# A decoder's state-space layer: channels projected once, the convolution as shifted taps on ScalarE and VectorE

## What is computed

```python
zxbcdt = x @ W_in.T
z, xBC, dt_raw = zxbcdt[..., :512], zxbcdt[..., 512:1280], zxbcdt[..., 1280:]
y = causal_conv(xBC, conv_w)          # per channel, 4 taps: positions t-3 .. t
xBC = y * sigmoid(y)
xs, B, C = xBC[..., :512], xBC[..., 512:640], xBC[..., 640:]
dt = softplus(dt_raw + dt_bias); cum = cumsum(-exp(A_log) * dt)
M[i, j, h] = (C_i . B_j) * exp(cum_i - cum_j) * dt_j      # j <= i, 64 heads of 8
y = einsum(M, xs) + D * xs
y = rms_norm(y * silu(z)) * norm_w
return y @ W_out.T
```

## Time and profile before

| | |
|---|---|
| median of 3 runs | 2465.02 us (2462.78 to 2465.8) |
| the profiled execution | 2466.13 us, its span 2464.3 us |
| PE / DVE / ACT / POOL busy over the span | 83% / 68% / 54% / 51% |
| mean granted clock of PE | 0.954 |
| state space | from about 1017.8 to 1482.5 us of the span |

### The profile page before, as it was taken

The page is one execution under the profiler, slowest core; times in us unless marked ns, Lnnn a source line. Parts: engine busy times, 40 slices in busy tenths (PEclk is TensorE's granted clock), DMA queues, the critical chain, the costliest instruction groups (busy, mean ns, idle before and its releaser), DMA issues. The chain is left out here.

```text
span 2464.3 us, 36286 instructions
## 1 busy us (share of the span) xinstructions
PE 2053.8 (83%) x10114; PEld 1341.9 (54%) x10114; DVE 1665.6 (68%) x3834; ACT 1322.8 (54%) x5017; POOL 1253.8 (51%) x1524
## 2 busy tenths in 40 slices
PE   0776999999999997498888870499999999999995
PEld 0453666566656655255555440266666666666664
DVE  7454566676676675466565658367888877888886
ACT  1223566666666664223232323277777777777773
POOL 0014444444454442155555564156777766777765
PEclk9997999999999999699999995699999999999998
DMA  5000000000000002000000005000000000000000
GB/s 198 0 0 16 5 3 3 4 2 2 4 2 2 2 0 74 1 1 0 0 0 0 0 0 197 15 3 3 6 8 6 5 7 5 5 7 5 3 5 8
DMA packets 30027, 37.35 MB, mean 15 GB/s; under 512 B 3281, under 2 KB 24273, under 8 KB 29265
## 3 DMA queue, kind: packets, MB, share of 16 engines
q1 hardware_dynamic: 29904, 36.11, 4.3%
HBM read 34.00 MB, written 2.10 MB: 15 GB/s over the span
## 5 line engine op out<-in xcount | busy, mean ns | idle before, releaser
L1092 POOL TENSOR_TENSOR ssm_y<-ssm_y,ssm_term 128x512 f32<-128x512 f32 x112 | 142.2, 1269 | 146.7 <-DVE ssm_term L1265 144.2
L1593 POOL TENSOR_TENSOR fa_rs<-fa_rs,all_minus_half 128x4 f32<-128x4 f32 x192 | 197.9, 1031 | 15.0
L1654 PE MATMUL fa_pJB<-fa_w_kvx,fa_ctxT 128*128 128x512 f32 x256 | 128.7, 628 | 80.0 <-DMA fa_ctxT<-in_ctxT 79.3
L1778 ACT ACTIVATE fa_qT<-fa_pH,fa_head_vec 128x512 f32<-128x512 f32 x128 | 99.5, 777 | 173.7 <-PE fa_pH L1753 173.7
L1787 ACT ACTIVATE fa_pS<-fa_pS,fa_nb 128x128 f32<-128x128 f32 x512 | 182.6, 392 | 7.1 <-issue 6.7
L1590 POOL TENSOR_TENSOR fa_rs<-fa_ms,all_eps5w 128x4 f32<-128x4 f32 x192 | 43.9, 229 | 242.1 <-ACT fa_q_junk L1771 129.6
L1673 PEld LDWEIGHTS fa_pS<-fa_kT,fa_qT 128*128 128x128 f32 x1024 | 123.9, 191 | 65.3 <-ACT fa_qT L1778 58.5
L1614 POOL TENSOR_TENSOR fa_cat<-fa_ov,fa_om 128x512 bf16<-128x512 f32 x128 | 153.7, 1200 | 5.3
L1673 PE MATMUL fa_pS<-fa_kT,fa_qT 128*128 128x128 f32 x1024 | 148.2, 288 | 2.5 <-ACT fa_qT L1778 0.9
L1607 POOL TENSOR_TENSOR fa_ov<-fa_ob,fa_om 128x512 f32<-128x512 bf16 x128 | 147.7, 1154 | 4.7 <-DVE fa_om L1960 4.7
L521 PE MATMUL xa_pS<-xa_kT,xa_qT 128*128 128x256 f32 x512 | 126.2, 388 | 23.2 <-ACT xa_kT L699 17.5
(11 more groups left out here) (329 smaller groups left out, 5971.3 us busy)
## 6 DMA issues: line engine op xcount, KB each, us to landing
faw_raw<-in_fa_w SPq DMA_DIRECT2D x12, 512.0 KB, 6.7
faw_raw<-in_fa_wproj SPq DMA_DIRECT2D x8, 512.0 KB, 3.9
all_X<-in_x SPq DMA_DIRECT2D x1, 2048.0 KB, 13.5
shared_weights<-in_xa_wq SPq DMA_DIRECT2D x1, 2048.0 KB, 13.4
xa_wo<-in_xa_wo SPq DMA_DIRECT2D x1, 2048.0 KB, 18.3
xa_ctxT<-in_ctxT SPq DMA_DIRECT2D x16, 128.0 KB, 2.1
fa_w_kvx<-in_fa_wkvx SPq DMA_DIRECT2D x1, 2048.0 KB, 14.8
fa_ctxT<-in_ctxT SPq DMA_DIRECT2D x16, 128.0 KB, 2.1
```

The lines of the kernel that those rows point to most:

```text
L1092: pool.tensor_tensor(y[:, side, :], y[:, side, :], term[:, in_turn(side, l), :], ALU.add)\
L1593: pool.tensor_tensor(rs[:, j % 2, cols], rs[:, j % 2, cols], env.mhalf[:, cols], ALU.pow)\
```

## The change

B, C and x are projected once, all with channels on partitions: two products a tile of 128 channels (`channels`, 2 tiles into `pC`, 4 into `pX`). ACT writes the newest tap of each tile from PSUM to a new SBUF tile `conv`, scaled by a value per channel (`first_tap`); DVE adds the three older taps, each a multiply-add of the PSUM tile, read 1 to 3 positions earlier, into `conv` (`tap`: 3 steps of 2 tiles for B and C, 3 steps of 4 tiles for x, each step behind a semaphore of the one before). ACT takes Silu of B and C from `conv` to `bcT`. x is transposed back by PE into `pX` (4 transposes) and goes through Silu as before. `w_tap`, its four multiplications, the copy `cur`, the zero columns and their clearing go; x is transposed straight from `env.X`. On PE z's product moves ahead of C.B, between levels 1 and 2. On DVE the taps of B and C stand ahead of term 2, those of x behind it, and C.B's masks behind term 3. The steps are written out, with no loop. The tap weights are loaded as [128, 6, 4] (12 KB) in place of a copy on each partition (1536 KB).

```diff
-            steps(0, 0, False, True)
-            steps(1, 1, True, True)
-            with eng.Fori(2, B - 1, 2) as m:
-                steps(m, 0, True, True)
-                steps(m + 1, 1, True, True)
-            steps(B, 0, True, False)
+            for m in range(B + 1):
+                steps(m, m % 2, m > 0, m < B)
...
+                    def channels(bank, tiles):
+                        for n, tile in enumerate(tiles):
+                            for k in range(KT):
+                                last = pe.matmul(bank[:, n * P:(n + 1) * P], w_raw[:, k, tile * P:(tile + 1) * P],
+                                                 xT[:, k, :], start=(k == 0), stop=(k == KT - 1))
+                        return last
...
-                        for half in range(2):
-                            for n in range(TAPS * KT):
-                                t, k = n // KT, n % KT
-                                last = pe.matmul(pC[:, half * N:(half + 1) * N],
-                                                 w_tap[:, t, k, HID + half * N:HID + (half + 1) * N],
-                                                 xT[:, k, t:t + P],
-                                                 start=(n == 0), stop=(n == TAPS * KT - 1))
-                        last.then_inc(s["bc_ps"], 1)
+                        channels(pC, (4, 5)).then_inc(s["bc_ps"], 1)
+                        pe.wait_ge(s["xs_in"], now(m, 0))
+                        channels(pX, (0, 1, 2, 3)).then_inc(s["xp_ps"], 1)
                     next_level()
+                    next_level()
+                    if front:
+                        for k in range(KT):
+                            last = pe.matmul(pZ[:, :], xT[:, k, :], w_z[:, k, :],
+                                             start=(k == 0), stop=(k == KT - 1))
+                        last.then_inc(s["z_ps"], 1)
                     next_level()
...
-                    for n in range(TAPS * KT):
-                        if n in (0, 2, 4, 5, 6):
-                            next_level()
-                        if front:
-                            last = tap(n)
+                    next_level()
+                    next_level()
                     if front:
+                        pe.wait_ge(x_tap, now(m + 1, 0, PAD, PAD - 1))
+                        for n in range(HID // P):
+                            last = pe.transpose(pX[:, n * P:(n + 1) * P], conv[:, n, :], env.ident[:])
                         last.then_inc(s["xs_ps"], 1)
+                    next_level()
+                    next_level()
...
+                def first_tap(ready, bank, tiles, done, m):
+                    act.wait_ge(s[ready], now(m, 0))
+                    for n, tile in enumerate(tiles):
+                        last = act.activation(conv[:, tile, :], bank[:, n * P:(n + 1) * P], ACT.Copy,
+                                              scale=conv_w[:, tile, PAD:PAD + 1])
+                    last.then_inc(s[done], 1)
...
-                        act.activation(cur[:], env.X[:, m, :], ACT.Copy).then_inc(s["cur_in"], 1)
...
+                        first_tap("bc_ps", pC, (4, 5), "bc_first", m + 1)
+                        first_tap("xp_ps", pX, (0, 1, 2, 3), "x_first", m + 1)
+                        act.wait_ge(bc_tap, now(m + 1, 0, PAD, PAD - 1))
+                        act.activation(bcT[:], conv[:, 4:6, :].rearrange("p n t -> p (n t)"), ACT.Silu)\
+                            .then_inc(s["bc_in"], 1)
...
+                def tap(t, bank, tiles, first, done, m):
+
+                    if t == PAD - 1:
+                        dve.wait_ge(s[first], now(m, 0))
+                    else:
+                        dve.wait_ge(done, now(m, 0, PAD, PAD - 2 - t))
+                    late = PAD - t
+                    for n, tile in enumerate(tiles):
+                        last = dve.scalar_tensor_tensor(out=conv[:, tile, late:P], in0=bank[:, n * P:(n + 1) * P - late],
+                                                        scalar=conv_w[:, tile, t:t + 1], in1=conv[:, tile, late:P],
+                                                        op0=ALU.mult, op1=ALU.add)
+                    last.then_inc(done, 1)
...
+                    if front:
+                        for t in reversed(range(PAD)):
+                            tap(t, pC, (4, 5), "bc_first", bc_tap, m + 1)
                     terms(2)
+                    if front:
+                        for t in reversed(range(PAD)):
+                            tap(t, pX, (0, 1, 2, 3), "x_first", x_tap, m + 1)
+                    terms(3)
...
-                    terms(3, 4, 5, 6)
+                    terms(4, 5, 6)
...
-                for tap in range(TAPS):
-                    dve.tensor_tensor(w_tap[:, tap], w_raw[:], conv_w[:, tap, :].unsqueeze(1)
-                                      .to_broadcast([P, KT, CONV]), ALU.mult)
```

More of the change, by code:

```diff
@@ L1011, in state_space @@
             "z", "dt", "bcx", "conv", "out", "norm", "dt_bias", "a_log", "d", "spans", "pairs")]
-        w_tap = sb("w_tap", [P, TAPS, KT, CONV])
-        cur = sb("cur", [P, D])
-        xT = sb("xT", [P, KT, PAD + P])
+        xT = sb("xT", [P, KT, P])
+        conv = sb("conv", [P, CONV // P, P])
         sz = sb("sz", [P, 2, HID])
@@ L1126, in level @@
                                   start=True, stop=True).then_inc(level_ps, 1)
-                    def tap(n):
-                        t, k = n // KT, n % KT
-                        return pe.matmul(pX[:, :], xT[:, k, t:t + P], w_tap[:, t, k, 0:HID],
-                                         start=(n == 0), stop=(n == TAPS * KT - 1))
+                    def channels(bank, tiles):
[4 more added lines that the diff above has]
+                        return last
                     levels = iter(range(LEVELS))
@@ L1140, in steps @@
                     if front:
-                        pe.wait_ge(s["cur_in"], now(m + 1, 0))
                         pe.wait_ge(s["z_in"], now(m, 0))
                         for k in range(KT):
-                            last = pe.transpose(pZ[:, k * P:(k + 1) * P], cur[:, k * P:(k + 1) * P], env.ident[:])
+                            last = pe.transpose(pZ[:, k * P:(k + 1) * P], env.X[:, m, k * P:(k + 1) * P], env.ident[:])
                         last.then_inc(s["xT_ps"], 1)
@@ L1148, in steps @@
                         for k in range(KT):
-                            last = pe.matmul(pE[:, 0:H], xT[:, k, PAD:PAD + P], w_dt[:, k, :],
+                            last = pe.matmul(pE[:, 0:H], xT[:, k, :], w_dt[:, k, :],
                                              start=(k == 0), stop=(k == KT - 1))
@@ L1210, in steps @@
                         act.activation(log_p[:], one_p[:], ACT.Ln).then_inc(s["log_done"], 1)
-                        act.wait_ge(s["bc_ps"], now(m + 1, 0))
-                        act.activation(bcT[:], pC[:, 0:2 * N], ACT.Silu).then_inc(s["bc_in"], 1)
+                        first_tap("bc_ps", pC, (4, 5), "bc_first", m + 1)
[3 more added lines that the diff above has]
+                            .then_inc(s["bc_in"], 1)
                         act.wait_ge(s["z_ps"], now(m + 1, 0))
```

24 lines of the change are left out of this document (8 added, 16 removed).

## The result

The changed kernel takes 2491.66 us (median of four executions, 2483.81 to 2499.4), the kernel before 2464.03 us (four, 2462.78 to 2465.8). The ratio is 1.0111, 95% interval 1.0073 to 1.015: slower by 1.1%. The forecast was 2460.5 us and its range ended at 2490, so the prediction is wrong in its direction, and the median lies 1.7 us outside the range (two of its four executions lie inside).

What follows compares the result with a forecast made beforehand. PE was taken to bound the stage (busy 370 of 428 us), DVE and POOL close behind. Start -10.5, steps +3.5 and PE's clock +2.5 gave -4.5 us, median 2465.02 to 2460.5; own range 2452 to 2471, whole range 2440 to 2490.

Steps and rivals of the forecast that it cites:

- (b): Step from term 0 at 11.00 us after the gate to the softplus's end at 15.04, if PE has level 0 by then.
- the clock's estimate: PE's clock falling in longer idle stretches: one step in four at 0.7 us, 15 x 0.17 = +2.5 us.
- Spare: 2.0 us: Slack before term 0 at 11.00: PE's level 0 issued at 7.95, its result at 9.0.
- The walk: Times through one step after the change, counted from the gate multiply: 27.68 us to the next gate, against 27.43 before.
- start: Start of the stage, without the four tap-weight multiplications on DVE: -10.5 us, bounds -7 and -12.
- steps, without the clock: The fourteen steps from gate to gate: 14 x (27.68 - 27.43) = +3.5 us.
- rival D: PE at 1.2 GHz for the projections in most steps, level 0 late for term 0: 2487, all steps 2526; chance 0.13.
- E: POOL's skip starts before DVE's gate multiply, which ends at 1.75 instead of 0.69: +0.2 x 14, 2463.3; chance 0.03.
- (a): Step from 0 to 9.28 us, gate multiply to next dt: unchanged, paced by DVE and POOL taking turns.
- rivals A, B and C: DVE's taps: cheap, 2442.5, chance 0.15; filling DVE's waits for nothing, 2380, chance 0.04; dear, 2497, chance 0.13.

Runs made afterwards that it cites:

- the first two kernels of the half change: Changed kernel with levels 0 and 1 first, skip after the gate, x's convolution back on PE: 2450.27 us; that with C.B before x's last four products: 2446.17 us.
- the fastest kernel: The second of the first two kernels of the half change, with x's products respread, five before C.B and one behind each of levels 4, 5, 6: 2409.34 us.
- skip late: The changed kernel with one edit, POOL's skip product waits for the gate multiply: 2460.44 us, ratio 0.9988.

## Why the prediction was wrong

**The step that failed is (b) with the clock's estimate: "Spare: 2.0 us", and beside it +0.17 us a step for the clock.** The walk put level 0 at 7.95 us after the gate; it is issued at 13.10, so 5.15 late, and term 0 3.16 late. The terms of the sum against what the traces show, in us:

| term | predicted | measured |
|---|---|---|
| start | -10.5 | -12.1 |
| steps, without the clock | +3.5 (27.68 a step) | +0.5 (27.47, with the gate's wait filled) |
| clock | +2.5 | +39.4 (424.01 - 14 x 27.47) |
| last step | in the walk | -0.7 |
| the rest of the kernel | 0 | +3.2 |
| sum | -4.5 | +30.4 |

Everything but one term is within 3.2 us. The clock's was off by a factor of sixteen. What the runs showed in its place: the clock stays low from 2 to 12 us after the gate in eleven of fourteen steps, because the gate multiply, held by skip, lengthens PE's wait to 3.04 us and makes everything behind it late. Filled with unread products (2458.57 us) or shortened by one wait on POOL (2460.44), that wait costs next to nothing.

**Its upper bound was in the text.** I had worked out what half clock through all of (b) does ("level 0 would be 4.4 us late"), and for half of it 0.7, and then took one step in four at the smaller price. The trace shows eleven of fourteen steps at 3 us and the rest at 0.3 to 1.1, which by the text's own prices is rival D, "2 us late in most steps gives +27 and 2487", and I gave it 0.13. Against it I had the row 90 to 120 with a clock of 1.00, where PE is idle a quarter of the time too; but the longest wait of PE in that row is 1.50 us, and those of this stage after the change are single ones of 3. The row that had a longer one, 1300 to 1310 at 0.83, was of this very stage: the clock fell at the end of a wait of 2.21 us, and that step took 28.97 where its neighbours took 27.11. I read it as a bound on the size instead of as the nearest case. Both slow steps of before, 28.81 and 28.97, have such a stretch of low clock in the trace.

**D and E were kept as separate cases.** E was read rightly as a mechanism: skip first, gate multiply held (its end was put at 1.75 us, measured 1.54). It was priced by what it does to DVE's chain (+0.2; 0.11 measured) and given 0.03. The walk in (a) said that PE's y transposes "come 0.2 us earlier; nobody gains"; they come at 1.60 and not at 0.74, as the held multiply is what they wait for. The prediction's idle time of PE around the gate, 2.3 us, is 3.04 before the y transposes and 0.69 behind them. The 0.97 us that the output product is later than the walk's 2.05 fits by itself into 2.0 of spare, and so do the 1.6 to 1.7 of half clock on the output product. Their sum isn't, since the delay also carries the next products into the low clock. The Trainium skill, SBUF — State Buffer, section "Summary: rules for kernel authors", says that of a DVE instruction with two SBUF inputs and a GpSimd one that reads SBUF the second to issue fully blocks; the trace agrees, with the multiply as the second by 0.08 us. E's chance was also too low. The text itself had "the gate multiply starts too" at the end of POOL's last addition; before, skip waited for ACT's xs, and this change takes that wait away. Skip, next on the same engine, starts 0.04 us before the addition's end, and the gate multiply, which waits for the addition on another engine, starts 0.04 after it, in all fifteen steps.

**What was right.** The mean of the multiply-adds is 339 to 344 ns where 350 was taken. Six take 1.88 us and twelve 3.41, 5.3 in all where the walk had 5.5. The walk from term 0 on was 16.68 us, measured 16.55; term 3, the masks and the additions of POOL stand where it put them. With the gate's order mended the step is 27.36 where the walk said 27.68 without the clock, so rivals A, B and C are out. The start: PE first at 1018.67 (said 1019.6), its own part -6.2 as said and 0.9 from the stage before; to the first decay Exp 14.8 (said 15.0); the first attend step cost nothing (said 0.5). The loop cost nothing, shown by the kernel written out. The forecast's 2460.5 is what the change gives with one more wait on POOL, 2460.44, but that is partly luck: a start better by 2 us and faster steps stand against a rest of the kernel that is 3.9 longer.

**What stays open.** The rest of the kernel, untouched, is longer by 1.8 to 4.0 us in after and its variants with x by channels. It is 1.1 and 0.9 shorter in the first two kernels of the half change, and 3.1 and 3.2 shorter in before written out and in the fastest kernel. No run was made for it. It need not come from the change: the kernel before, 29 times on one chip, ran from 2458.14 us at a mean clock of 0.958 to 2466.47 at 0.953, so a single profile can differ by as much. Why a few steps of after escape (27.93, 29.09, 28.52) while the others repeat to 0.02 us was not tested; in those DVE waits 0.3 to 1.1 us for term 0, and the clock is back by 6.0 to 8.5 us after the gate and not by 12. That the clock follows PE's idle time is shown for the wait at the gate (filled, it doesn't fall there, but for the steps of 29.47); how far it depends on what ran before that wait is not.

## What to carry to other kernels

Before work is taken off the bound engine, walk its new waits and ask of each what runs right behind it and who waits for that: a low clock is free behind one wait and costs 3 us a step behind another. Costs that each fit into a spare must be added up before they are compared with it, and work that nobody needs yet doesn't go ahead of a product that another engine waits for. Moving only that part of the work which leaves both chains equal (six multiply-adds a step instead of eighteen, and PE's own products spread over its waits) gave what the whole move lost.

## What the runs showed of the hardware

- Of the two operations that POOL's last addition lets go, the one that is next on POOL starts first: skip 0.08 us ahead of DVE's gate multiply, and the multiply takes 1.54 us for 0.69 in all fifteen steps. With the order turned, the hold moves to the decay product behind (3.04 us for 2.29), where it is nearly free.
- The granted clock is low from 1.8 to 2.1 until 12.0 to 12.3 us after the gate multiply's start in the slow steps of after, and only until 5.2 to 5.8 in the fast steps with skip late, where PE's wait for the gate is 2.19 us and not 3.04.
- Four unread products of 256 columns before a wait of 3 us save 33 us in the kernel (30 by the ratios); six before a wait that nobody depends on save nothing that can be told from none.
- The same mean clock of 0.84 goes with steps of 30.29 us and of 27.43.
- A multiply-add of 125 to 127 columns from PSUM with a scalar per partition takes 339 to 344 ns, one of 128 columns without such a scalar 281; ACT's scaled copy of 128 columns takes 354 to 370 ns (all three in the profile of after or before).
- The steps written out run as fast as a loop over them: 1.0005, 0.9994 to 1.0015.
